# Local correlation on tiles of 8 rows by 16 columns instead of 4 whole rows

## The chip, the cores and the metric

The kernel runs on one core of a Trainium2 chip. The metric is the device time of one execution in microseconds; less is better. The times and the profile are of single executions; the table below has both.

## The reference

Eight images of 512 channels and 32x32 pixels go through two layers. With v = groupnorm(x), 32 groups of 16 channels:

```python
norm = sqrt(sum(v * v, axis=1, keepdims=True))
fn = v / maximum(norm, 1e-12)
fp = pad(fn, 2 pixels on each side)
vol = stack([sum(fp[:, :, r:h + r, cc:w + cc] * fn, axis=1)
             for cc in range(5) for r in range(5)], axis=1)     # 25 channels
x = x + relu(einsum('bihw,oi->bohw', concat([v, vol], axis=1), conv_w) + conv_b)
```

So each pixel is multiplied with its 25 neighbours over 512 channels, the 25 products are divided by the two norms, and a 1x1 convolution takes 512 + 25 channels to 512. All is float32.

## The kernel before

The work is 16 units, one image in one layer each (`ORDER`); four units lie in a ring of operand tiles. `KT` = 4 tiles of 128 channels, `PIX` = 1024 pixels. A float32 value is held as two float16 parts, high and low, so a convolution matmul is done three times (L442: `wh` with high, `wl` with high, `whh` with low). The order on every engine is written out by hand, and semaphores join them. In step k the engines do:

- TensorE: the correlation products of unit k (L453 to L472), then for the convolution of unit k-1 eight groups g of 12 matmuls with 512 columns (`channels`, L442) and one volume product (`volume`, L449), which adds the 25 correlation channels. The volume products of g = 0 and 1 come behind the 24 matmuls of these groups, since `vol` is late (`HOLD` = 1). At g = 2 stands the group average for unit k+1 (L420), at g = 4 the turning of unit k's neighbours (L494).
- ScalarE: eviction of the correlation products to `band` (L556), `vol` high part (L544), and between the ReLUs (L594) the high parts of unit k+1 (L536, from g = 2) and half of the turned rows (L587).
- VectorE: statistics of unit k+1 (`unit_stats`, L625), the low part of `vol` of unit k-1 (L689), the affine values (`unit_affine`, L646 to L670) at g = 0, norms and neighbours of unit k (L696 to L720) at g = 2, then per g one tile of unit k+1: `v` (L678) and the low part (L683). After each g's part comes the residual addition (L792). The copy of the other half of the turned rows (L728) comes at g = 4 behind the tile t = 2.
- SP: `band` to DRAM, and back skewed into `skew` (L284); outputs and new x tiles; the turned rows to DRAM (L289).
- GpSimd: three views of these rows from DRAM (L359 to L365) and three products with them (L378 to L383), whose result `corr` becomes `vol`.

The correlation works so: a block is 128 pixels, 4 whole rows. Its pixels are the weights (128 columns of `opnd`, high part); the moving operand is the 4 rows with 2 more above and below, 8 x 32 = 256 columns, with high and low part, for 4 channel tiles: 8 matmuls per block, 64 per unit. In the result [pixel, column] pixel i needs columns i to i + 132. `band` goes to DRAM row by row and is read back with a step one longer than a row, so that each partition gets its own window of `REACH` = 133 values for each of 8 blocks. `nbr` takes 25 of them and 25 mirrored ones; the borders of the image are rid of later through the padded rows.

GpSimd clears what is never written (L332 to L337); all engines wait for these constants.

Of the kernel before, what the change touches and what calls it, by code (L numbers as in the profile page):

```python
# [61 lines left out]
def build(nc, x, w0, b0, w1, b1, out):  # L62
# [8 lines left out]
    ROWS = P // WI  # L71
    BLOCKS = PIX // P
    BAND = (ROWS + 2 * R) * WI
    PAIRS = BLOCKS // 2
    REACH = 2 * R * WI + S
    CENTRE = R * WI + R
# [6 lines left out]
    GPAD = 64  # L83
    GSZ = GPAD + BLOCKS * P * BAND + GPAD
    GROUPS = 2 * KT
    BN = 6
    assert (B, UNITS) == (BATCHES, B * LAYERS) and BAND * 2 == HALF
# [7 lines left out]
    with ctx:  # L95
        def sb(name, shape, dt):
            return ctx.enter_context(nc.sbuf_tensor(name, shape, dt))
# [20 lines left out]
        band = sb("band", [P, PAIRS, HALF], F32)  # L118
# [39 lines left out]
        pads_out = sem("pads_out")  # L158
# [15 lines left out]
        low = sem("low")  # L174
        gram = sem("gram")
# [17 lines left out]
        CONSTS = 11  # L193
# [21 lines left out]
        def valid(u):  # L215
            return 0 <= u < UNITS

# [19 lines left out]
        def _(sp):  # L237
# [35 lines left out]
            def band_through_dram(k, q):  # L273

                for p in range(PAIRS):
                    sp.wait_ge(band_sb, PAIRS * k + p + 1)
                    dst = bass.AP(band_dram, q * GSZ + GPAD + 2 * p * P * BAND,
                                  [[BAND, P], [P * BAND, 2], [1, BAND]])
                    sp.dma_start(dst, band[:, p, :].rearrange("p (a n) -> p a n", a=2)).then_inc(band_out, 16)
# [3 lines left out]
                src = bass.AP(band_dram, q * GSZ + GPAD - R, [[BAND + 1, P], [P * BAND, BLOCKS], [1, REACH]])  # L283
# [34 lines left out]
        def _(pool):  # L318
# [14 lines left out]
            pool.memset(band[:, 0, 0:R * WI], 0.0).then_inc(const_step, 1)  # L333
            pool.memset(band[:, PAIRS - 1, HALF - R * WI:HALF], 0.0).then_inc(const_step, 1)
# [78 lines left out]
        def _(pe):  # L413
# [38 lines left out]
            def step(k, k0, i):  # L452
                if valid(k0):  # L453
                    slot = k0 % RING
                    pe.wait_ge(high, KT * (k + 1))
                    pe.wait_ge(low, KT * (k + 1))
                    if k0 == 2:
                        pe.wait_ge(w_low, W_LOWS * LAYERS)
                    for p in range(PAIRS):
                        wait(pe, band_sb, PAIRS * k + p - 1)  # L460
                        for j in range(2 * p, 2 * p + 2):
                            r0 = max(ROWS * j - R, 0)
# [354 lines left out]
```

## Time and profile before

| | |
|---|---|
| median of 3 runs | 570.47 us (570.29 to 570.53) |
| the profiled execution | 571.38 us, its span 569.5 us |
| TensorE granted clock, mean | 0.974 |
| busy: TensorE, VectorE, ScalarE, GpSimd | 502.5, 408.0, 258.7, 165.4 us |
| DMA | 69.43 MB, mean 122 GB/s |

The span is from the first to the last instruction. In the rows below, "PE" is TensorE's matmuls, "PEld" its weight loads, "DVE" VectorE, "ACT" ScalarE, "POOL" GpSimd, "SPq" the queue of SyncE that issues DMAs; L12 is line 12 of the kernel. A matmul's shown duration holds the pipeline's latency: the distance from start to start is what one costs. A busy share says nothing of what sets the end; that is in the chain and in the waits.

### The profile page before, as it was taken

To read this page: it belongs to the slowest core of one execution; us is meant where nothing else is said; L and a number is where in the kernel's file an instruction comes from. 1 tells how busy PE (TensorE), PEld (TensorE's weight loads), DVE (VectorE), ACT (ScalarE), POOL (GpSimd) and SP (SyncE) were. 2 spreads that over 40 slices of the span, in tenths; PEclk is the share of its full clock that TensorE was granted. 3 is DMA by queue.
4 is the path that set the end of the run, shared out by engine and by line. 5 is a ranking of instruction groups with operands and counts; after the bars stand their busy time and mean duration, and the time that the engine had idled before them with its cause. 6 is when DMAs were issued, how large, how long until landed. Compare 5 with 4: busy or idle time off the path is not lost.

```text
span 569.5 us, 7778 instructions
## 1 busy us (share of the span) xinstructions
PE 502.5 (88%) x2888; PEld 284.8 (50%) x2888; DVE 408.0 (72%) x828; ACT 258.7 (45%) x350; POOL 165.4 (29%) x135
## 2 busy tenths in 40 slices
PE   0357779999999989998999989998999989998996
PEld 0246337454564646454464636455464646454442
DVE  4879696786869588785969588785958778572442
ACT  1343454644546363643545364543646263543332
POOL 3354625023140504114140503214040503214240
PEclk9976989999999989999999989999999999999999
DMA  8764202223133812455043712356041512334403
GB/s 332 265 208 129 70 1 75 73 54 95 30 117 138 262 43 73 132 199 186 14 133 122 268 54 72 114 199 206 9 137 75 181 39 71 114 121 136 145 37 148
DMA packets 49885, 69.43 MB, mean 122 GB/s; under 512 B 6248, under 2 KB 39016, under 8 KB 49848
## 3 DMA queue, kind: packets, MB, share of 16 engines
q1 hardware_dynamic: 46008, 63.42, 33.1%
q0 software_dynamic: 3840, 5.52, 4.1%
q8 instruction: 23, 0.38, 0.3%
q14 instruction: 14, 0.11, 0.1%
HBM read 33.21 MB, written 35.71 MB: 121 GB/s over the span
## 4 chain that ended last, share of the span: by engine, by line
PE 34%; DVE 23%; issue 14%; POOL 14%; DMA 9%; ACT 5%; DVEq 0%; POOLq 0%
PE conv_ps L442 24%; DVE xs L792 5%; PE gram_ps L467 5%; DMA xs<-in_x_dram 4%; POOL corr L383 3%; POOL mirror L378 3%; DVE v L678 3%; POOL corr L381 3%; PE conv_ps L449 3%; DMA rows_dram<-rows 3%; DVE vol L689 2%; ACT act_out L594 2%; DMA out_dram<-xs 2%; DVE opnd L683 2%; DVE stats L625 2%
## 5 line engine op out<-in xcount | busy, mean ns | idle before, releaser
L442 PE MATMUL conv_ps<-opnd,wh 128*128 128x512 f16 x512 | 195.9, 383 | 0.2 <-ACT act_out L594 0.2
L442 PE MATMUL conv_ps<-opnd,whh 128*128 128x512 f16 x512 | 196.0, 383 | 0.0
L442 PE MATMUL conv_ps<-opnd,wl 128*128 128x512 f16 x512 | 195.9, 383 | 0.0
L594 ACT ACTIVATE act_out<-conv_ps,bias,wdown 128x512 f32<-128x512 f32 x128 | 97.4, 773 | 118.9 <-PE conv_ps L449 117.5
L792 DVE TENSOR_TENSOR xs<-xs,act_out 128x512 f32<-128x512 f32 x128 | 92.2, 736 | 44.8 <-ACT act_out L594 44.5
L467 PE MATMUL gram_ps<-opnd 128*128 128x256 f16 (+1 forms) x1024 | 111.1, 271 | 13.7 <-DVE opnd L683 11.7
L467 PEld LDWEIGHTS gram_ps<-opnd 128*128 128x128 f16 x1024 | 98.8, 100 | 27.6 <-issue 14.2
L625 DVE BATCH_NORM_STATS2 stats<-xs 128x6 f32<-128x512 f32 x128 | 78.3, 679 | 25.1 <-DMA xs<-in_x_dram 19.1
L359 POOL DMA_DIRECT2D mirror<-rows_dram x16 | 10.5, 659 | 273.3 <-DMA rows_dram<-rows 273.3
L683 DVE SCALAR_TENSOR_TENSOR opnd<-opnd,v 128x1024 f16<-128x1024 f16 x64 | 80.8, 1266 | 10.3 <-POOL v L390 4.1
L442 PEld LDWEIGHTS conv_ps<-opnd,whh 128*128 128x128 f16 x512 | 50.3, 98 | 61.8 <-issue 2.1
L536 ACT ACTIVATE opnd<-xs,affine 128x1024 f16<-128x1024 f32 x64 | 78.2, 1230 | 4.9 <-DVE affine L670 4.9
L442 PEld LDWEIGHTS conv_ps<-opnd,wh 128*128 128x128 f16 x512 | 51.5, 101 | 56.6 <-issue 2.1
L442 PEld LDWEIGHTS conv_ps<-opnd,wl 128*128 128x128 f16 x512 | 50.4, 98 | 56.3 <-issue 2.1
L556 ACT ACTIVATE band<-gram_ps 128x448 f32<-128x448 f32 (+1 forms) x64 | 36.5, 571 | 74.1 <-PE gram_ps L467 74.1
L449 PE MATMUL conv_ps<-vol,wvol 96*128 96x512 f16 x128 | 45.9, 381 | 17.3 <-DVE vol L689 14.4
L544 ACT ACTIVATE vol<-corr 25x1024 f16<-25x1024 f32 x32 | 33.8, 1055 | 51.4 <-POOL corr L383 51.0
L378 POOL TENSOR_TENSOR mirror<-mirror,rn_own 25x1024 f32<-25x1024 f32 x16 | 37.7, 2357 | 60.4 <-DMA rn_own<-rows_dram 60.4
L689 DVE SCALAR_TENSOR_TENSOR vol<-corr,vol 25x1024 f16<-25x1024 f32 x16 | 19.8, 1236 | 40.1 <-ACT vol L544 39.9
L678 DVE TENSOR_SCALAR v<-xs,affine 128x1024 f32<-128x1024 f32 x56 | 45.4, 811 | 0.0
L383 POOL TENSOR_TENSOR corr<-corr,mirror 25x1024 f32<-25x1024 f32 x16 | 37.9, 2366 | 1.3
L381 POOL TENSOR_TENSOR corr<-rows,rn_far 25x1024 f32<-25x1024 f32 x16 | 32.9, 2058 | 0.0
(67 smaller groups left out, 245.9 us busy)
## 6 DMA issues: line engine op xcount, KB each, us to landing
xs<-in_x_dram SPq DMA_DIRECT2D x32, 512.0 KB, 4.7
band_dram<-band SPq DMA_DIRECT2D x64, 256.0 KB, 2.3
out_dram<-xs SPq DMA_DIRECT2D x32, 512.0 KB, 2.9
skew<-band_dram SPq DMA_DIRECT2D x16, 532.0 KB, 4.0
opnd<-in_L_conv_conv_w_dram SPq DMA_DIRECT2D x2, 1074.0 KB, 12.5
rows_dram<-rows SPq DMA_DIRECT2D x16, 131.6 KB
mirror<-rows_dram POOLq DMA_DIRECT2D x16, 112.1 KB, 2.3
rn_far<-rows_dram POOLq DMA_DIRECT2D x16, 112.1 KB, 3.8
```

The lines of the kernel that those rows point to most:

```text
L378: pool.tensor_tensor(mir, mir, near, ALU.mult).then_inc(corr_step, 1)
L381: pool.tensor_tensor(dst, own, far, ALU.mult).then_inc(corr_step, 1)
L383: pool.tensor_tensor(dst, dst, mir, ALU.add).then_inc(corr_step, 1)
L442: pe.matmul(conv_ps[:, g % 4, :], w[:, l, t, m * P:(m + 1) * P], opnd[:, slot, part, t, n * HALF:(n + 1) * HALF], start=(t == 0 and w is w ...
L449: pe.matmul(conv_ps[:, g % 4, :], wvol[0:96, l, m * P:(m + 1) * P], vol[0:96, n * HALF:(n + 1) * HALF], start=False, stop=True).then_inc(c ...
L467: last = pe.matmul(gram_ps[:, p % 2, at:at + (r1 - r0) * WI], opnd[:, slot, 0, t, j * P:(j + 1) * P], opnd[:, slot, part, t, r0 * WI:r1 * WI],
L536: act.activation(opnd[:, u0 % RING, 0, t, :], xt, ACT.Identity, bias=affine[:, 0, 1, t:t + 1], scale=affine[:, 0, 0, t:t + 1]).then_inc(hi ...
L594: act.activation(act_out[:, g % 2, :], conv_ps[:, g % 4, :], ACT.Relu, bias=bias[:, l, m:m + 1], scale=wdown[:, l, m:m + 1]).then_inc(relu, 1)
L625: last = dve.bn_stats(stats[:, t, h, :], xs[:, slot, t, h * HALF:(h + 1) * HALF])
L678: dve.tensor_scalar(v2[:, t % 2, :], xs[:, ring_slot(unit_batch(k0 + 1) + 2 * i), t, :], affine[:, 1, 0, t:t + 1], affine[:, 1, 1, t:t + 1 ...
L683: dve.scalar_tensor_tensor(out=opnd[:, slot, 1, t, :], in0=opnd[:, slot, 0, t, :], scalar=-2.0, in1=v2[:, t % 2, :], op0=ALU.mult, op1=ALU ...
L792: dve.tensor_tensor(xt, xt, act_out[:, g % 2, :], ALU.add).then_inc(x_sum, 1)
```

## The change

A block becomes a tile of 8 rows by 16 columns: 4 tiles down, 2 across, still 8 blocks and 64 matmuls. The moving operand is 12 rows of 18 columns (`HELD`: 16 and 2 on the inner side; the other side is the image's border), 216 columns, or 180 at the upper and lower edge, picked from the image with a step of 32. [...] `band` holds 12 x 20 values per tile with zeros at the border, all of it cleared at the start. In DRAM the two tiles of a pair lie beside each other, 480 values per pixel, with pitches such that pixel i again reads with a constant step; each window is 85 values. The four writes of pads to DRAM go. ScalarE's eviction, the turning's target (L494) and the neighbour step (L717) follow the layout. The reserve for DMA descriptors is cut to 4096 bytes per partition, which makes room for `strips`.

```diff
+    TR, TC = 8, 16
+    DOWN, ACROSS = HI // TR, WI // TC
+    BLOCKS = DOWN * ACROSS
+    BR, BC = TR + 2 * R, TC + 2 * R
+    BAND = BR * BC
+    PAIRS = DOWN
+    REACH = 2 * R * BC + S
+    WL_PITCH = BLOCKS * BAND + 4
+    HL_PITCH = TC * (WL_PITCH + 1) - BC
+    GSZ = TR * HL_PITCH + TC
+    HELD = TC + R
...
+        strips = sb("strips", [P, KT, ACROSS, HI * TC], F16)
...
-            for q in range(2):
-                sp.dma_start(band_dram[q:q + 1, 0:GPAD], rows[0:1, 0:GPAD]).then_inc(pads_out, 16)
-                sp.dma_start(band_dram[q:q + 1, GSZ - GPAD:GSZ], rows[0:1, 0:GPAD]).then_inc(pads_out, 16)
-            sp.wait_ge(pads_out, 64)
...
-                    dst = bass.AP(band_dram, q * GSZ + GPAD + 2 * p * P * BAND,
-                                  [[BAND, P], [P * BAND, 2], [1, BAND]])
+                    dst = bass.AP(band_dram, q * GSZ + p * ACROSS * BAND,
+                                  [[HL_PITCH, TR], [WL_PITCH, TC], [1, ACROSS * BAND]])
...
-                src = bass.AP(band_dram, q * GSZ + GPAD - R, [[BAND + 1, P], [P * BAND, BLOCKS], [1, REACH]])
+                src = bass.AP(band_dram, q * GSZ, [[WL_PITCH + 1, P], [BAND, BLOCKS], [1, REACH]])
...
-            pool.memset(band[:, 0, 0:R * WI], 0.0).then_inc(const_step, 1)
-            pool.memset(band[:, PAIRS - 1, HALF - R * WI:HALF], 0.0).then_inc(const_step, 1)
+            pool.memset(band[:, :, :], 0.0).then_inc(const_step, 1)
...
+                    pe.wait_ge(stripped, KT * (k + 1))
...
-                                    last = pe.matmul(gram_ps[:, p % 2, at:at + (r1 - r0) * WI],
-                                                     opnd[:, slot, 0, t, j * P:(j + 1) * P],
-                                                     opnd[:, slot, part, t, r0 * WI:r1 * WI],
+                                    last = pe.matmul(gram_ps[:, p % 2, c * HALF // 2:c * HALF // 2 + HELD * (r1 - r0)],
+                                                     strips[:, t, c, p * P:(p + 1) * P],
+                                                     image(opnd[:, slot, part, t, :])[:, r0:r1, c0:c0 + HELD],
...
-                        act.activation(band[:, p, a:z], gram_ps[:, p % 2, a:z], ACT.Copy).then_inc(band_sb, 1)
+                        r0, r1 = held_rows(p)
+                        bp, gp = band[:, p, :], gram_ps[:, p % 2, :]
+                        dst = bass.AP(bp.tensor, bp.offset + (r0 - (p * TR - R)) * BC + R,
+                                      [list(bp.ap[0]), [BAND - R, ACROSS], [BC, r1 - r0], [1, HELD]])
+                        src = bass.AP(gp.tensor, gp.offset,
+                                      [list(gp.ap[0]), [HALF // 2, ACROSS], [HELD, r1 - r0], [1, HELD]])
+                        act.activation(dst, src, ACT.Copy).then_inc(band_sb, 1)
...
                 dve.wait_ge(high, KT * u + t + 1)
+                wait(dve, gram, PAIRS * u)
+                dve.tensor_copy(strips[:, t, :, :].rearrange("p c (h w) -> p c h w", w=TC),
+                                opnd[:, slot, 0, t, :].rearrange("p (h c w) -> p c h w", c=ACROSS, w=TC)
+                                ).then_inc(stripped, 1)
                 dve.wait_ge(twice, KT * u + t + 1)
...
-    nc = _bacc.Bacc("TRN2", target_bir_lowering=False, num_devices=1)
+    nc = _bacc.Bacc("TRN2", target_bir_lowering=False, num_devices=1, dynamic_dma_scratch_size=4096)
```

## Rows read from the trace of the kernel before

**Rows 1.** The page: engines' busy time (section 1) and the chain's shares (section 4).

```profile
PE 502.5 (88%) x2888; PEld 284.8 (50%) x2888; DVE 408.0 (72%) x828; ACT 258.7 (45%) x350; POOL 165.4 (29%) x135
PE 34%; DVE 23%; issue 14%; POOL 14%; DMA 9%; ACT 5%; DVEq 0%; POOLq 0%
```

**Rows 2.** Chain of work in time: start us, us, what, number.

```profile
92.94 6.56 PE gram_ps L467 x64
...
350.21 6.56 PE gram_ps L467 x64
```

**Rows 3.** Waits, 92 to 524 us: engine, line, releaser: total us, times, longest.

```profile
PE conv_ps L449 <- DVE vol L689: 14.4, 11, 2.7
```

**Rows 4.** Timeline of VectorE, one round: start, us, instruction [idle before, releaser].

```profile
457.28 1.21 DVE L689 SCALAR_TENSOR_TENSOR vol<-corr,vol 25x1024 f16<-25x1024 f32 x1 [3.33 <-ACT vol L544]
459.39 0.17 DVE L646 COPY gmv<-turn_ps 128x8 f32<-128x8 f32 x1 [0.90 <-PE turn_ps L420]
...
465.42 0.81 DVE L678 TENSOR_SCALAR v<-xs,affine 128x1024 f32<-128x1024 f32 x1
466.33 1.22 DVE L683 SCALAR_TENSOR_TENSOR opnd<-opnd,v 128x1024 f16<-128x1024 f16 x1
467.47 0.68 DVE L792 TENSOR_TENSOR xs<-xs,act_out 128x512 f32<-128x512 f32 x1
...
472.78 0.68 DVE L728 COPY rows<-turn_ps 90x512 f32<-90x512 f32 x1
...
488.62 1.21 DVE L689 SCALAR_TENSOR_TENSOR vol<-corr,vol 25x1024 f16<-25x1024 f32 x1 [3.33 <-ACT vol L544]
```

**Rows 5.** Windows: length, busy PE, PEld, DVE, ACT, POOL (instructions), clock, DMA.

```profile
461.90:473.50 11.60, 11.03 (x56) 5.30 (x54) 10.84 (x21) 8.11 (x10) 0.00 (x0) 1.00 0.00 0
```

**Rows 6.** Timeline of VectorE at the end of a round with an x load.

```profile
197.39 1.29 DVE L625 BATCH_NORM_STATS2 stats<-xs 128x6 f32<-128x512 f32 x2 [1.94 <-DMA xs<-in_x_dram]
...
199.64 1.22 DVE L689 SCALAR_TENSOR_TENSOR vol<-corr,vol 25x1024 f16<-25x1024 f32 x1
```

**Rows 7.** Timeline of TensorE: the first volume products of three rounds.

```profile
167.84 0.59 PE L449 MATMUL conv_ps<-vol,wvol 96*128 96x512 f16 x2 [0.70 <-DVE vol L689]
...
201.00 0.59 PE L449 MATMUL conv_ps<-vol,wvol 96*128 96x512 f16 x2 [2.18 <-DVE vol L689]
...
523.61 0.59 PE L449 MATMUL conv_ps<-vol,wvol 96*128 96x512 f16 x2 [2.67 <-DVE vol L689]
```

**Rows 8.** Prices: first eight correlation matmuls (timeline); L678 (groups by shape: busy, mean ns).

```profile
123.69 0.82 PE L467 MATMUL gram_ps<-opnd 128*128 128x192 f16 x8
...
L678 DVE TENSOR_SCALAR v<-xs,affine 128x1024 f32<-128x1024 f32 x56 | 45.4, 811 | 0.0
```

**Rows 9.** Timeline of GpSimd and VectorE at the start.

```profile
2.33 1.18 POOL L332 MEMSET rows<- 90x1296 f32 x1
3.45 0.15 POOL L333 MEMSET band<- 128x64 f32 x1
...
5.80 4.85 DVE L625 BATCH_NORM_STATS2 stats<-xs 128x6 f32<-128x512 f32 x8 [5.80 <-POOL nbr L337]
...
16.11 3.25 DVE L683 SCALAR_TENSOR_TENSOR opnd<-opnd,v 128x1024 f16<-128x1024 f16 x2 [1.44 <-POOL v L390]
```

**Rows 10.** The skewed read: page's DMA issues (KB, us to landing), timelines of SP and VectorE.

```profile
skew<-band_dram SPq DMA_DIRECT2D x16, 532.0 KB, 4.0
...
200.10 0.36 SPq L284 DMA_DIRECT2D skew<-band_dram  x1
...
205.47 0.16 DVE L696 TENSOR_SCALAR nsq<-skew 128x8 f32<-128x8 f32 x1
...
454.63 0.36 SPq L284 DMA_DIRECT2D skew<-band_dram  x1
```

**Rows 11.** Windows behind two of these waits, columns as in rows 5 (clock: third from the end).

```profile
201.90:205.30 3.40, 3.40 (x10) 1.21 (x8) 2.62 (x13) 1.05 (x3) 0.00 (x0) 0.50 0.45 136
...
523.60:527.00 3.40, 3.39 (x16) 1.57 (x17) 1.82 (x6) 1.66 (x3) 0.00 (x0) 1.00 0.00 0
```

More of the change, by code:

```diff
@@ L82, in build @@
     MIR = (HI - 1) * PW + WI
-    GPAD = 64
-    GSZ = GPAD + BLOCKS * P * BAND + GPAD
+    WL_PITCH = BLOCKS * BAND + 4
+    HL_PITCH = TC * (WL_PITCH + 1) - BC
+    GSZ = TR * HL_PITCH + TC
+    HELD = TC + R
     GROUPS = 2 * KT
     BN = 6
-    assert (B, UNITS) == (BATCHES, B * LAYERS) and BAND * 2 == HALF
+    assert (B, UNITS) == (BATCHES, B * LAYERS) and BAND * 2 <= HALF and ACROSS == 2 and TR * TC == P
     weights = (w0, w1)
@@ L115, in build @@
         wvol = sb("wvol", [P, LAYERS, C], F16)
+        strips = sb("strips", [P, KT, ACROSS, HI * TC], F16)
         vol = sb("vol", [P, PIX], F16)
         v2 = sb("v2", [P, 2, PIX], F32)
-        band = sb("band", [P, PAIRS, HALF], F32)
+        band = sb("band", [P, PAIRS, ACROSS * BAND], F32)
         skew = sb("skew", [P, BLOCKS, REACH], F32)
@@ L174, in build @@
         low = sem("low")
+        stripped = sem("stripped")
         gram = sem("gram")
@@ L191, in build @@
         x_sum = sem("x_sum")
-        CONSTS = 11
+        CONSTS = 10
         BN_STEPS = KT + KT + 2
@@ L216, in valid, with image, held_rows @@
             return 0 <= u < UNITS
+        def image(a):
+            return a.rearrange("p (h w) -> p h w", w=WI)
+        def held_rows(p):
+            return max(p * TR - R, 0), min((p + 1) * TR + R, HI)
         def w_turned_at(l, n):
@@ L460, in step @@
                         wait(pe, band_sb, PAIRS * k + p - 1)
-                        for j in range(2 * p, 2 * p + 2):
-                            r0 = max(ROWS * j - R, 0)
-                            r1 = min(ROWS * (j + 1) + R, HI)
-                            at = (j % 2) * BAND + (r0 - (ROWS * j - R)) * WI
+                        r0, r1 = held_rows(p)
+                        for c in range(ACROSS):
+                            c0 = 0 if c == 0 else WI - HELD
                             for t in range(KT):
                                 for part in range(2):
-                                    last = pe.matmul(gram_ps[:, p % 2, at:at + (r1 - r0) * WI],
-                                                     opnd[:, slot, 0, t, j * P:(j + 1) * P],
-                                                     opnd[:, slot, part, t, r0 * WI:r1 * WI],
+                                    last = pe.matmul(gram_ps[:, p % 2, c * HALF // 2:c * HALF // 2 + HELD * (r1 - r0)],
+                                                     strips[:, t, c, p * P:(p + 1) * P],
+                                                     image(opnd[:, slot, part, t, :])[:, r0:r1, c0:c0 + HELD],
                                                      start=(t == 0 and part == 0),
@@ L493, in step @@
                         for j in range(BLOCKS):
-                            last = pe.transpose(turn_ps[0:NROWS, j * P // HALF, j * P % HALF:j * P % HALF + P],
+                            h, c = j // ACROSS, j % ACROSS
+                            last = pe.transpose(image(turn_ps[0:NROWS, h // 2, :])[:, h % 2 * TR:(h % 2 + 1) * TR,
+                                                                                  c * TC:(c + 1) * TC],
                                                 nbr[:, j, :], ident[:, :])
```

15 lines of the change are left out of this document (4 added, 11 removed).

## The prediction

> **What bounds the kernel now.** I read the page first. TensorE is busy 88% of the span and VectorE 72%, but of the chain that ended last TensorE has only 34%, VectorE 23%, GpSimd 14% and DMA 9% [rows 1]: a loop over several engines ends the rounds, not TensorE's work alone. Next the chain in order of time. A correlation block of 64 matmuls (L467) should stand on it 16 times if its length mattered in every unit; it stands there four times (23.96, 92.94, 221.15 and 350.21 us), the second and the last shown in [rows 2]. Then the waits between 92 and 524 us: TensorE waits in 11 rounds for vol of L689 before it can do the volume product L449 [rows 3].
>
> So I followed one round on VectorE [rows 4]. L689 at 457.28 writes vol, TensorE does L449 and the group average, and from the copy L646 at 459.39 VectorE has a queue that hardly breaks: affine steps, two residual additions, norms, neighbours, then tiles of the next unit (L678, L683, one addition L792 each), and only behind the third tile, at 472.78, the copy of turned rows L728. Between 461.9 and 473.5 it is busy 10.84 us of 11.60, the rest being the gaps between dependent small steps [rows 5]. The copy ends at 473.46. Then comes a leg without a TensorE matmul in it: rows to DRAM, three views back, three GpSimd products, ScalarE's vol, until L689 starts at 488.62, 15.16 us later. The round is 31.34 us: 2.11 + 14.07 + 15.16. L467 is in none of the three parts. TensorE runs beside it, and waits for it.
>
> There is a second kind of round: four in which a new x tile is loaded. There the last loads hold the statistics (L625), and L689 stands behind these in VectorE's queue [rows 6]. Such a round, from L449 at 167.84 to L449 at 201.00 [rows 7], has 33.16 us, with TensorE waiting 2.18 us at its end. The path is TensorE's products, output, load, statistics. The correlation block is not on it either: it runs beside the output and the load.
>
> **The change part by part.**
>
> *Correlation matmuls.* Columns per unit: before 48 of 256 and 16 of 192, 15360. After 12 rows of 18 are 216, at the upper and lower edge 10 rows of 18 are 180: 32 x 216 + 32 x 180 = 12672. 64 matmuls in 6.56 us [rows 2] are 102.5 ns each, and the first eight of 192 columns take 0.82 us with their tail [rows 8]; both fit one column per 1/2.4 ns plus 2.5 ns. So the block becomes 32 x 92.5 + 32 x 77.5 ns = 5.44 us, a saving of 1.12 us per unit, 17.9 us over 16 units. By the above it is worth nothing where TensorE waits for vol; it is worth 1.1 us at unit 2 (92.94), a few tenths for the first unit, and lengthens the wait elsewhere. Bounds: 192-column matmuls are the shortest of their kind here; if 180 costs as much as 192 (82.5 ns) the saving is 0.96. That strided runs of 18 are slower shows nowhere and is a rival.
>
> *The strips.* Four new VectorE copies per unit, 128x1024, f16 to f16, each between L678 and L683 of its tile. The nearest row by size and by its single tensor source is L678: 811 ns, f32 [rows 8]. The floor is the 128x8 copy L646, 170 ns [rows 4]. Half the bytes of L678: 170 + (811 - 170) / 2 = 490 ns, an estimate, which I take. What it adds is less. L683 waits for L678 today: it starts 0.91 us after it though L678 has 0.81 [rows 4], and independent neighbours overlap by 0.08 us (L683 has 1.22 and the next addition starts 1.14 later). Tile now: 0.91 to L683. Tile then: 0.73 + 0.41 = 1.14. So +0.23 us per copy; +0 at the floor, +0.55 at 811 ns, and +0.97 at 1.22 us, the duration of L683 at one element per cycle. Three of the four stand ahead of L728, in a queue with no slack: +0.7 us per round. The fourth is hidden: VectorE later waits for ScalarE and for vol.
> The Trainium skill, "VectorE: DVE Perf Modes", perf-mode tier table, gives a 16-bit copy within SBUF four elements per cycle. By it I estimate 0.42 us per copy, 0.16 added, 0.5 per round, and a total 2 us lower than below. No row here has a 16-bit VectorE copy.
>
> The rounds it counts in are those whose L689 waits for the leg behind L728. From unit 2 to unit 14 there are thirteen; four are load rounds, and a load round has room against a plain one (33.16 beside 31.34: 1.8 us) that takes up 0.7. Nine rounds x 0.7 = 6.3 us. The tail behind unit 14 has no next unit, no copy and no correlation block: 0.
>
> *Start.* The two small clears of band (0.15 us each, L333, L334) become one of 1920 f32 per partition. L332 clears 1296 in 1.18 us, so 1.75 us, 1.45 more. The first statistics wait for these constants with all x tiles there (idle 5.80, then eight without a break) [rows 9]: +1.45, all of it on the path. SP loses the four pads and their landing, ahead of load(2), whose tiles are not waited for: 0. In units 0 and 1 GpSimd computes v beside VectorE, and there L683 takes 3.25 us for two instead of 2.4 [rows 4, 9]: the engines get in each other's way. The copies partly fill idle time and partly wait behind GpSimd: between 0 and 3 us over both units, I take 1.0. The four tiles of unit 2 stand on the chain behind 66.7 us: +0.9, against the 1.1 of unit 2's shorter block: 0 together.
>
> *Eviction and DMA.* L556 writes 432 and 360 columns instead of 512 and 448, in the shadow of the block: 0. Band goes out as 1920 B per partition instead of twice 1024; skew comes back in 1024 chunks of 340 B instead of 532. Skew lands after 4.0 us, the median [rows 10]. In a plain round it is issued at 454.63 and has landed when the affine steps begin at 459.39, and the norms come behind these [rows 4, 10]. Behind a load round it is issued at 200.10 and read at 205.47: 1.4 us of room. I take no change: 0; double would cost there (rival). The smaller reserve for descriptors touches three small GpSimd DMAs per unit: 0, bounds -0.3 to +0.3 us per unit.
>
> *The clock.* TensorE's wait at L449 grows in plain rounds by 1.1 + 0.7 us, in load rounds by 1.1. Granted clock after a wait of 2.18 us: 0.50 for 3.4 us; after one of 2.67 us at 523.61: 1.00 [rows 7, 11]. So a wait of over 2 us may or may not halve the clock (1.2 instead of 2.4 GHz), which costs 1.7 us of TensorE's time. Where the next wait swallows that it is free. It isn't at unit 14: the wait becomes 4.5 us, and TensorE is the bound from there to the end: +1.7. In each of four load rounds it could cost 1.7 as well, if the plain round before it ends in a halved clock: 0 to 6.8, in the range only.
>
> Sum on the profiled execution (569.5 span, 1.9 around it, 571.4): 1.45 + 1.0 + 0 + 6.3 + 1.7 = +10.4, so 581.8. The median is 0.9 under the profiled run: **581.0**.
>
> **The rivals.**
> 1. *The copy is slow*, one element per cycle (1.22 us). For: 16-element pieces from two interleaved halves. Price: 9 x 2.9 in plain rounds, 4 x 1.1 in load rounds, 3.9 less 1.1 at unit 2, 5 for the start and the clock: 38 us, 609 with the 0.9 off. 0.10.
> 2. *Strided matmuls are slow.* If a column costs double, the block takes 10.9 us, 4.3 more than now; TensorE's 0.4 to 0.7 of wait goes and every round grows by 3.7: 13 x 3.7 + 3 = 51 on 570.5, 621. Against: the rows of 36 bytes are read in order. 0.05.
> 3. *Skew's small chunks.* If the landing doubles to 8 us, the four rounds behind loads lose 4.0 - 1.4 = 2.6: +10, 591. The Trainium skill, "DMA: Bandwidth & Descriptors", Specifications, wants 512 B per transfer for full rate, with read-modify-write below it; 532 is above and 340 below, so by that rule this rival holds. Against: a third less data. 0.08.
> 4. *Faster.* The copy vanishes in the gap in which L683 waits for L678, and the shorter block counts where TensorE or shared DMA time sets the end: first unit -0.3, unit 2 -1.1, four load rounds -0.8 each with less band traffic beside the load, against 1.45: -3.2, 567. It decides if a copy adds under 0.05 us. If, besides, TensorE were the real bound in all rounds, 553. Against: the waits of [rows 3]. 0.05.
>
> **How the numbers follow.** Forecast 0.67, rivals 0.28, the rest (GpSimd at the start, descriptors) 0.05. Copy at its floor, with nothing for the clock or the crowding at the start: 1.45 less 1.1 on 570.5, 571; with both, 574. Copy at 811 ns: 9 x 1.65 + 1.1 (unit 2) + 1.45 + 3 + 1.7 = 22.1, 593. Range 574 to 594, which holds the forecast with its clock terms and rival 3; rivals 1, 2 and 4, 0.20 together, are outside. Differences under about 0.2% (1.1 us) can't be told from none. Faster 0.07 (rival 4 and a part of the rest), same 0.05 (the copy at its floor or below), slower 0.88.
>
> **What would show it.** Right: 5.4 us for the 64 matmuls of a unit; copies of 0.4 to 0.5 us; the copy of turned rows 0.5 to 0.7 us later behind L646; a longer wait for vol at the volume product; first statistics 1.45 later; load rounds of the same length. Wrong: matmuls that take more than their columns, a copy of turned rows that is not later, norms that wait for skew, or a correlation block on the chain in most units.

## The result, and the profile after

The changed kernel takes 584.06 us (median of 4 runs, 581.12 to 584.57) against 570.5 us: 1.0219 times the kernel before, interval 1.0179 to 1.0260. On another chip it was 1.0205 (1.0175 to 1.0235), against a median of 571.69 us there. The forecast was 581.0, range 574 to 594, slower. The profiled execution took 584.57 us with a span of 582.5, so the two spans differ by 13.0 us.

The page of the changed kernel: section 1, the granted clock by slice, the chain's shares, and three groups of section 5.

```profile
PE 495.4 (85%) x2888; PEld 280.7 (48%) x2888; DVE 421.6 (72%) x892; ACT 255.0 (44%) x350; POOL 170.0 (29%) x134
...
PEclk9986899999999989997999989998999989997999
...
DVE 31%; POOL 19%; PE 18%; issue 15%; DMA 9%; ACT 6%; SPq 1%; DVEq 0%; POOLq 0%
...
L456 PE MATMUL conv_ps<-vol,wvol 96*128 96x512 f16 x128 | 47.0, 391 | 32.6 <-DVE vol L706 31.3
...
L696 DVE COPY strips<-opnd 128x1024 f16<-128x1024 f16 x64 | 26.9, 420 | 3.2 <-ACT opnd L545 3.2
...
skew<-band_dram SPq DMA_DIRECT2D x16, 340.0 KB, 3.3
```

TensorE's share of the chain went from 34% to 18% [rows 1], and VectorE's and GpSimd's rose, from 23% to 31% and from 14% to 19%. Its wait for vol at the volume product (L456 now, L449 before) went from 14.4 us in 11 waits [rows 3] to 31.3 in 13. The correlation block stands on the chain in time only twice now (four times before, [rows 2]):

```profile
97.05 5.52 PE gram_ps L474 x64
...
190.63 5.54 PE gram_ps L474 x64
```

So it shrank from 6.56 us to 5.53, which over 16 units is 16.5 us, and the wait for vol grew by 16.9. The change does what it says on TensorE, and all of it is waited away again. TensorE's busy time fell by 7.1 us only (502.5 to 495.4), since more of its work ran at the half clock: the mean granted clock went from 0.974 to 0.957.

VectorE in a plain round of the changed kernel, the timeline; L706 is L689 before, L659 is L646, L745 is L728, L691 is L678, L700 is L683, and L696 is the new copy of a channel tile's high part into `strips`, from which TensorE now takes its weights.

```profile
432.95 1.21 DVE L706 SCALAR_TENSOR_TENSOR vol<-corr,vol 25x1024 f16<-25x1024 f32 x1 [3.33 <-ACT vol L553]
435.06 0.17 DVE L659 COPY gmv<-turn_ps 128x8 f32<-128x8 f32 x1 [0.90 <-PE turn_ps L427]
...
438.78 0.16 DVE L713 TENSOR_SCALAR nsq<-skew 128x8 f32<-128x8 f32 x1
...
441.12 0.80 DVE L691 TENSOR_SCALAR v<-xs,affine 128x1024 f32<-128x1024 f32 x1
441.84 0.42 DVE L696 COPY strips<-opnd 128x1024 f16<-128x1024 f16 x1
442.17 1.22 DVE L700 SCALAR_TENSOR_TENSOR opnd<-opnd,v 128x1024 f16<-128x1024 f16 x1
443.31 0.68 DVE L809 TENSOR_TENSOR xs<-xs,act_out 128x512 f32<-128x512 f32 x1
...
448.90 0.68 DVE L745 COPY rows<-turn_ps 90x512 f32<-90x512 f32 x1
...
466.35 1.22 DVE L706 SCALAR_TENSOR_TENSOR vol<-corr,vol 25x1024 f16<-25x1024 f32 x1 [3.51 <-ACT vol L553]
```

From the start of L659 to that of L745 it is 13.84 us; from L646 to L728 it was 13.39 [rows 4]: +0.45 for three copies. A tile takes 1.05 us from L691 to L700 (442.17 less 441.12) and not 0.91, so a copy adds 0.14 to 0.15 us though it has 0.42: it fills part of the gap in which L700 waited for L691.

Where the 13.0 us came from, by the start of the first volume product of each unit in the timelines of TensorE. The last column is from the trace of the same kernel on the other chip, with a span of 584.0 us:

| Stretch | before | after | difference | second trace |
|---|---|---|---|---|
| start to unit 0 | 66.73 | 70.20 | +3.47 | +4.28 |
| unit 0 to 1 | 37.79 | 37.63 | -0.16 | +0.01 |
| nine plain rounds, 1 to 14 | 287.84 | 292.46 | +4.62 | +6.33 |
| four load rounds, 3-4, 5-6, 7-8, 9-10 | 131.25 | 133.58 | +2.33 | +1.32 |
| unit 14 to the end | 45.84 | 48.62 | +2.78 | +2.6 |

So one trace fixes the size of a stretch to no better than 1 to 2 us.

### The profile page after: what moved, and what is told of

Read it like the earlier page. It is cut to its first block, busy times and chain, and to the rows that moved or that the text cites. A ratio compares the mean times of both kernels' runs of the same rounds, so it can differ in the third digit from the quotient of the medians.

```text
span 582.5 us, 7851 instructions
## 1 busy us (share of the span) xinstructions
PE 495.4 (85%) x2888; PEld 280.7 (48%) x2888; DVE 421.6 (72%) x892; ACT 255.0 (44%) x350; POOL 170.0 (29%) x134
## 3 DMA queue, kind: packets, MB, share of 16 engines
q1 hardware_dynamic: 37296, 59.22, 31.1%
## 4 chain that ended last, share of the span: by engine, by line
DVE 31%; POOL 19%; PE 18%; issue 15%; DMA 9%; ACT 6%; SPq 1%; DVEq 0%; POOLq 0%
PE conv_ps L449 13%; DVE opnd L700 6%; DVE xs L809 5%; POOL mirror L385 5%; POOL corr L390 5%; DVE v L691 4%; POOL corr L388 4%; DMA rows_dram<-rows 4%; DMA band_dram<-band 3%; ACT vol L553 2%; DVE vol L706 2%; ACT act_out L607 2%; PE gram_ps L474 2%; PE conv_ps L456 2%; DVE stats L638 2%
## 5 line engine op out<-in xcount | busy, mean ns | idle before, releaser
L449 PE MATMUL conv_ps<-opnd,wh 128*128 128x512 f16 x512 | 199.8, 390 | 0.2 <-ACT act_out L607 0.2
L449 PE MATMUL conv_ps<-opnd,whh 128*128 128x512 f16 x512 | 199.2, 389 | 0.0
L449 PE MATMUL conv_ps<-opnd,wl 128*128 128x512 f16 x512 | 199.0, 389 | 0.0
L809 DVE TENSOR_TENSOR xs<-xs,act_out 128x512 f32<-128x512 f32 x128 | 88.4, 708 | 43.9 <-ACT act_out L607 43.9
L474 PE MATMUL gram_ps<-opnd,strips 128*128 128x180 f16 (+1 forms) x1024 | 94.3, 253 | 15.3 <-DVE opnd L700 15.3
L474 PEld LDWEIGHTS gram_ps<-opnd,strips 128*128 128x128 f16 x1024 | 91.7, 98 | 19.6 <-issue 15.8
L449 PEld LDWEIGHTS conv_ps<-opnd,whh 128*128 128x128 f16 x512 | 51.0, 100 | 64.3 <-issue 6.5
L700 DVE SCALAR_TENSOR_TENSOR opnd<-opnd,v 128x1024 f16<-128x1024 f16 x64 | 79.6, 1244 | 1.9 <-POOL v L397 1.9
L449 PEld LDWEIGHTS conv_ps<-opnd,wh 128*128 128x128 f16 x512 | 52.6, 103 | 58.6 <-issue 5.4
L449 PEld LDWEIGHTS conv_ps<-opnd,wl 128*128 128x128 f16 x512 | 51.2, 100 | 58.6 <-issue 6.0
L456 PE MATMUL conv_ps<-vol,wvol 96*128 96x512 f16 x128 | 47.0, 391 | 32.6 <-DVE vol L706 31.3
L569 ACT ACTIVATE band<-gram_ps 128x360 f32<-128x360 f32 (+1 forms) x64 | 32.4, 507 | 62.1 <-PE gram_ps L474 62.1
L706 DVE SCALAR_TENSOR_TENSOR vol<-corr,vol 25x1024 f16<-25x1024 f32 x16 | 19.8, 1236 | 43.4 <-ACT vol L553 43.3
L691 DVE TENSOR_SCALAR v<-xs,affine 128x1024 f32<-128x1024 f32 x56 | 45.5, 812 | 0.0
L456 PEld LDWEIGHTS conv_ps<-vol,wvol 96*128 96x128 f16 x128 | 11.6, 98 | 51.3 <-ACT vol L553 29.9
## 6 DMA issues: line engine op xcount, KB each, us to landing
opnd<-in_L_conv_conv_w_dram SPq DMA_DIRECT2D x2, 1074.0 KB, 12.8
```

The costliest lines, as they stand in the source:

```text
L449: pe.matmul(conv_ps[:, g % 4, :], w[:, l, t, m * P:(m + 1) * P], opnd[:, slot, part, t, n * HALF:(n + 1) * HALF], start=(t == 0 and w is w ...
L456: pe.matmul(conv_ps[:, g % 4, :], wvol[0:96, l, m * P:(m + 1) * P], vol[0:96, n * HALF:(n + 1) * HALF], start=False, stop=True).then_inc(c ...
L474: last = pe.matmul(gram_ps[:, p % 2, c * HALF // 2:c * HALF // 2 + HELD * (r1 - r0)], strips[:, t, c, p * P:(p + 1) * P], image(opnd[:, sl ...
L691: dve.tensor_scalar(v2[:, t % 2, :], xs[:, ring_slot(unit_batch(k0 + 1) + 2 * i), t, :], affine[:, 1, 0, t:t + 1], affine[:, 1, 1, t:t + 1 ...
L700: dve.scalar_tensor_tensor(out=opnd[:, slot, 1, t, :], in0=opnd[:, slot, 0, t, :], scalar=-2.0, in1=v2[:, t % 2, :], op0=ALU.mult, op1=ALU ...
L809: dve.tensor_tensor(xt, xt, act_out[:, g % 2, :], ALU.add).then_inc(x_sum, 1)
```

## The experiments

Ratios are to the kernel before on the same chip, over five rounds each, with their interval. Names of lines are those of the kernel from which the edit starts.

### The parts of the change alone

**The clear of band.** The kernel before, with the first of its two small clears made 1920 f32 long:

```diff
-            pool.memset(band[:, 0, 0:R * WI], 0.0).then_inc(const_step, 1)
+            pool.memset(band[:, :, :].rearrange('p a n -> p (a n)')[:, 0:1920], 0.0).then_inc(const_step, 1)
```

> The kernel before, with one edit: the first clear of band writes 1920 float32 values per partition, as the change does, instead of 64. Nothing else changes. Theory: the constants are done about 1.45 us later, the first statistics of VectorE start at 7.25 us instead of 5.80, and all of it reaches the end: 572.0 us. Rival: the x tiles or the weights set the start, and the time stays at 570.5.

Measured 1.0039 (1.0012 to 1.0067), about 2 us, with the first volume product 1.59 us later. In the changed kernel the same is seen on GpSimd and VectorE (timelines), 1.47 us later than in [rows 9]:

```profile
3.45 1.70 POOL L341 MEMSET band<- 128x1920 f32 x1
...
7.27 4.85 DVE L638 BATCH_NORM_STATS2 stats<-xs 128x6 f32<-128x512 f32 x8 [7.27 <-POOL nbr L344]
```

**The copies.** The kernel before, with the four copies in front of L683 and the smaller descriptor reserve; nothing reads the strips, and the correlation matmuls are the old ones:

```diff
                 dve.wait_ge(high, KT * u + t + 1)
+                wait(dve, gram, PAIRS * u)
+                dve.tensor_copy(strips[:, t, :, :].rearrange("p c (h w) -> p c h w", w=16),
+                                opnd[:, slot, 0, t, :].rearrange("p (h c w) -> p c h w", c=2, w=16)
+                                ).then_inc(stripped, 1)
...
+                    pe.wait_ge(stripped, KT * (k + 1))
```

> The kernel before with the four copies per unit into strips added on VectorE, at the place where the change has them, and the smaller reserve for DMA descriptors; the copies are waited for and not used, the correlation block keeps its 4-row blocks. Theory (VectorE's queue ahead of the copy of turned rows sets the round): 0.42 us per copy, 0.14 us added each, the copy of turned rows 0.4 us later behind the group average in every round, nine plain rounds x 0.4 = 3.8 us, and 2 to 3 us at the start, where the copies meet GpSimd's work: 576 to 577 us, TensorE's wait for vol longer by 0.4 in plain rounds. Rival (TensorE's own work is the bound, or the copies fall into gaps): within 1 us of 570.5.

Measured 1.0173 (1.0137 to 1.0210), 9.9 us, where 6 were expected. The copies take 422 ns here (groups by shape):

```profile
L686 DVE COPY strips<-opnd 128x1024 f16<-128x1024 f16 x64 | 27.0, 422 | 3.2 <-ACT opnd L539 3.2
```

The first volume product comes 1.85 us later, units 1 to 14 take 423.3 us instead of 419.1 (2.5 us of it in the nine plain rounds, 1.7 in the load rounds), and the tail 47.54 instead of 45.84: a fall of the clock behind unit 14's wait, which the expectation didn't have. So the copies alone make most of the slowdown; with the clear it is 2.1%. The shorter block, the new stores and the new read together come to about nothing, within some 3 us by these intervals.

**The copies moved behind the queue.** The changed kernel, with the copies of tiles 0 to 2 behind the copy of turned rows (L745) from unit 2 on:

```diff
...
+                    last_copied = TURN_AT(k0) if k0 > 1 else -1
+                    if 0 <= t < KT and valid(k0 + 1) and g > last_copied:
+                        strip_tile(k, k0, t)
+                    if g == last_copied and valid(k0 + 1):
+                        for s in range(t + 1):
+                            strip_tile(k, k0, s)
```

> The changed kernel with the same four VectorE copies per unit, but from the third step on those of tiles 0 to 2 stand behind the copy of turned rows instead of ahead of it. No work is taken away. Theory (only the queue ahead of that copy counts): the copy of turned rows ends 14.8 to 14.9 us behind the volume product instead of 15.3, nine plain rounds become 0.4 us shorter, 3 to 4 us in all: 580 to 581 us. Rival (it is the amount of VectorE work, wherever it stands): no change, 584.

Measured 1.0092 (1.0058 to 1.0125), a median of 576.5 us, 4 us lower than expected. From the first volume product to the turned rows' end it is 14.85 us again in most rounds (15.27 in the changed kernel, 14.82 before), units 1 to 14 take 421.0 us, and the tail is 45.87 us: the clock did not fall there, which the expectation had left out. So it is their place in the queue that costs, more than their 27 us of work. Over the clear's 2 us some 3 are left; in the trace the plain rounds are as short as before (287.3 us for 287.84) and the load rounds 2.5 us longer.

**ScalarE copies the strips.** The changed kernel with the four copies on ScalarE, two groups of the convolution later than the tile's high part:

```diff
+                act.wait_ge(high, KT * u + t + 1)
+                act.activation(strips[:, t, :, :].rearrange("p c (h w) -> p c h w", w=TC),
+                               opnd[:, u0 % RING, 0, t, :].rearrange("p (h c w) -> p c h w", c=ACROSS, w=TC),
+                               ACT.Copy).then_inc(stripped, 1)
...
-                dve.tensor_copy(strips[:, t, :, :].rearrange("p c (h w) -> p c h w", w=TC),
```

> The changed kernel with the four copies into strips on ScalarE instead of VectorE, 1.2 us each, from the third step on two groups later than the tile, in gaps where ScalarE waits for TensorE. Theory: the copy of turned rows ends 14.8 us behind the volume product again, nine plain rounds lose 0.4 us each and the start 1 to 2 us: 4 to 6 us less than the changed kernel, ratio to the kernel before 1.012 to 1.015. Rival (the copy itself costs little, the rest of the change is what is slow): ratio 1.02 as for the changed kernel.

Measured 1.0044 (1.0018 to 1.0069), where 1.012 to 1.015 was expected. A copy takes 1048 ns on ScalarE, and yet the kernel is 1.7% faster than with 420 ns on VectorE. The clear, and in the trace a tail of 47.55 us, are most of what is left over the kernel before.

### Is TensorE hidden, and what is its saving worth?

**The queue's last tile moved.** In both kernels the copy of turned rows (L728, L745) is put ahead of the third tile of the next unit, not behind it:

```diff
-                    if k0 == 0 and g == TURN_AT(k0):
+                    if (k0 == 0 or k0 > 1) and g == TURN_AT(k0) and valid(k0):
                         first_rows(k)
...
-                    if k0 != 0 and g == TURN_AT(k0) and valid(k0):
+                    if k0 == 1 and g == TURN_AT(k0) and valid(k0):
```

> The kernel before with one move: from the third step on VectorE's copy of turned rows stands ahead of tile t = 2 instead of behind it, so ahead of one v step and one low step (0.91 + 1.14 us). Theory (the round is: VectorE's queue up to this copy, then the leg through DRAM, GpSimd and ScalarE): the copy ends 12.8 us behind the volume product instead of 14.8, TensorE's wait for vol vanishes in plain rounds and these shrink from 31.6 to TensorE's own 30.8 us; load rounds stay at 32.4 to 33.2. Nine x 0.8 = 7 us less: ratio 0.988. Rival (TensorE's work or the DMA sets all rounds already): ratio 1.00.

> The changed kernel with the same move of the copy of turned rows ahead of tile t = 2 (and its strips copy). Theory (the shorter correlation block is worth something only where TensorE is the bound): the copy ends 12.9 us behind the volume product, TensorE becomes the bound of plain rounds with 29.8 us, one less than in the kernel before with this move; nine rounds x 2.0 us less than the changed kernel, and fewer falls of the clock: 562 to 566 us where the kernel before has 570.5, ratio 0.985 to 0.992, 2 to 4 us under the kernel before with this move (nine us won by the block, less 3.4 at the start and longer waits in load rounds). Rival (the change is slow for another reason, the matmuls or DMA): it stays 10 us above the kernel before with this move.

Measured: the kernel before with it 0.9816 (0.9782 to 0.9850), better than the 0.988 expected, the changed kernel with it 0.9926 (0.9898 to 0.9954). I had expected the changed kernel to come out lower of the two, by 2 to 4 us; it is 6 us above. The waits of TensorE at the volume product, the former kernel first, then the latter:

```profile
PE conv_ps L449 <- DVE vol L689: 7.3, 5, 2.0
```

```profile
PE conv_ps L456 <- DVE vol L706: 20.3, 14, 3.8
```

In the kernel before, TensorE waited for vol in seven of the nine plain rounds, 0.4 to 0.7 us in five of them. With turned rows 2.04 us sooner (14.82 to 12.78 behind the volume product) most plain rounds are 30.81 us long with no wait for vol, so that is TensorE's own work. Four of the five waits left are those of rounds that end with an x load; the fifth is 0.2 us at unit 14. In the changed kernel TensorE would need 29.8 (an estimate, 30.81 less the 1.03 of the block), but the median of its plain rounds is 31.1: first volume product to turned rows is 13.08 us and not 12.78, and behind that GpSimd's part begins later. Its DMA issue of mirror takes 1108 ns there in the mean and 659 in the kernel before (groups of lines, the changed kernel with the edit first):

```profile
L366 POOL DMA_DIRECT2D mirror<-rows_dram x16 | 17.7, 1108 | 262.4 <-DMA rows_dram<-rows 262.4
```

```profile
L359 POOL DMA_DIRECT2D mirror<-rows_dram x16 | 10.5, 659 | 273.3 <-DMA rows_dram<-rows 273.3
```

It isn't that VectorE is busy: it is busy all through the issue in the two kernels without the edit as well, and there the mean is 659 and 658 ns, with the copies and without them. What differs is the instruction that runs beside it. In those two it is the low part and an addition. With the edit it is `v`, and in the changed kernel the copy behind it. GpSimd's and VectorE's timelines of the changed kernel with the edit:

```profile
154.72 1.62 POOL L366 DMA_DIRECT2D mirror<-rows_dram  x1 [17.90 <-DMA rows_dram<-rows]
...
155.10 0.80 DVE L691 TENSOR_SCALAR v<-xs,affine 128x1024 f32<-128x1024 f32 x1
155.82 0.41 DVE L696 COPY strips<-opnd 128x1024 f16<-128x1024 f16 x1
```

The issue ends at 156.34, 0.11 us behind the copy (156.23). In the kernel before with the edit, where `v` stands alone, such an issue takes 1.14 us and ends 0.11 us behind `v`; the others take 0.65. This holds in six rounds of each of the two kernels with the edit; in the combination below one issue beside the start of `v` took 0.65 us all the same. So a longer issue goes with `v` and the copy beginning beside it. That they hold it up is read from these times, and no run tests it by itself.

**Both moves.** The changed kernel with the strips on ScalarE, the turned rows ahead of the third tile, and the clear of band behind the other constants, with only the first eviction waiting for it:

```diff
-            pool.memset(band[:, :, :], 0.0).then_inc(const_step, 1)
...
             pool.memset(nbr[:, :, NS:BACK], 0.0).then_inc(const_step, 1)
+            pool.memset(band[:, :, :], 0.0).then_inc(const_step, 1)
...
-            dve.wait_ge(const_step, CONSTS)
+            dve.wait_ge(const_step, CONSTS - 1)
...
+                            if k0 == 0:
+                                act.wait_ge(const_step, CONSTS)
```

> The changed kernel with three edits: the copies into strips on ScalarE, the copy of turned rows ahead of tile t = 2, and the clear of band as the last of GpSimd's constants, for which only ScalarE waits, ahead of its first band. Theory: the start comes back by 1.45 and 1 to 2 us, TensorE is the bound of plain rounds with 29.8 us: 558 to 562 us where the kernel before has 570.5, ratio 0.98 to 0.985. Rival (with TensorE at the bound the band's slower way through DRAM, 4.8 to 5.4 us from the last store's issue to the skewed read's instead of 2.1, takes its place): ratio above 0.99, norms that wait for skew in plain rounds.

Measured 0.9720 (0.9686 to 0.9753), better than the 0.98 to 0.985 expected, and 0.9744 (0.9714 to 0.9775) when it ran again on another chip, some 557 us. It beats both kernels, and the kernel before with its turned rows moved (562.7) by 5 us. Its chain (the page) has TensorE at half:

```profile
PE 52%; DMA 16%; DVE 14%; issue 6%; POOL 6%; ACT 4%; SPq 1%; DVEq 0%; POOLq 0%; ACTq 0%
```

Plain rounds at its start take 29.96 and 30.11 us, below the 30.81 that TensorE needs with the old block. Of the kernels run, only this one has time from the smaller block.

### The clock

**Dummy matmuls ahead of the wait.** The changed kernel with eight matmuls of 512 columns, whose result nobody reads, in front of TensorE's wait for vol:

```diff
                     if g == hold:
+                        if k0 > 2:
+                            pe.wait_ge(rows_a, k)
+                            for _ in range(WARM):
+                                pe.matmul(turn_ps[:, 1, :], wh[:, 0, 0, 0:P], opnd[:, slot, 0, 0, 0:HALF],
+                                          start=True, stop=True)
                         pe.wait_ge(vol_high, 2 * (u + 1))
```

> The changed kernel, with eight more matmuls of 512 columns on TensorE ahead of the wait for vol in each round from the third on; they write a bank that nothing reads then (a result of no use) and wait for ScalarE's copy of it, done long before. They take 1.7 us of the 2.0 to 4.8 us in which TensorE waits there. Theory (the waits make the granted clock fall to 0.50 behind six of the rounds): no fall behind these rounds, the last round of 31.28 us comes back to about 28.5, the plain rounds behind load rounds lose 0.4 to 0.9: 4 to 6 us less than the changed kernel, 578 to 580 us. Rival (the clock costs nothing, the loads vary): the same time as the changed kernel, or more where the eight matmuls are longer than the wait.

Measured 1.0241 (1.0197 to 1.0284): missed. The half clock behind the waits was gone but for one, but in unit 15, where TensorE is the bound, the dummies themselves stood in the way (1.73 us). So once more with none in that unit (`if 2 < k0 < UNITS`), beside the changed kernel itself:

> The changed kernel once more, unchanged, so that the next two runs have it on the same chip. Both theories: 1.022 times the kernel before (about 584 us), nine plain rounds of 31.8 to 32.1 us and a last full round (units 14 to 15) of 31.3 us with the matmuls of turn T and of the correlation block partly at half clock.

> The changed kernel with eight dummy matmuls (512 columns each, to a PSUM tile that nobody reads) ahead of the wait for vol, from unit 3 to unit 14 and none in the last step, where TensorE is the bound. Theory A, the fall of the clock behind unit 14's wait costs 2.8 us in the last full round: no half clock there, V14 to V15 28.5 instead of 31.3, and a few tenths behind each load round, 3 to 4 us under the changed kernel, near 580. Theory B, the clock is free, because the norms' wait for skew and the queues set the rounds: within 1 us of the changed kernel, and what the last round gains is lost before.

Measured 1.0205 (1.0175 to 1.0235) without and 1.0214 (1.0175 to 1.0253) with dummies: medians of 583.67 and 583.99 us. Windows behind the wait of unit 14, in the changed kernel as profiled first, and with the dummies:

```profile
532.70:539.50 6.80, 5.63 (x14) 2.09 (x15) 4.27 (x11) 2.51 (x4) 0.00 (x0) 0.50 0.27 99
```

```profile
532.70:539.50 6.80, 5.17 (x24) 2.36 (x25) 4.71 (x12) 3.73 (x6) 0.00 (x0) 1.00 0.40 127
```

In the traces it does what it should: clock 1.00 for 0.50, unit 14 to the end 45.86 us instead of 48.46 in the trace beside it, while unit 14 starts within 1.2 us. In the medians nothing of it is left. The runs of either spread over 4 to 6 us, and a gain of 2.6 may lie in it. That the other executions had no half clock to lose is unlikely: the mean granted clock is 0.948 to 0.960 in all six without dummies and 0.964 to 0.980 in all six with them. Where the time goes instead stays open. The theory that the clock is worth 3 to 4 us of median is not borne out.

### The stores of band

The stores are fewer bytes than before and are slower. SP's timeline in one plain round of the kernel before and of the changed one (the DMAs out of band, then the skewed read, which waits for them):

```profile
126.00 5.38 SPq L279 DMA_DIRECT2D band_dram<-band  x4
133.15 0.36 SPq L284 DMA_DIRECT2D skew<-band_dram  x1
```

```profile
128.89 4.84 SPq L287 DMA_DIRECT2D band_dram<-band  x4
137.98 0.38 SPq L292 DMA_DIRECT2D skew<-band_dram  x1
```

From the end of the last issue to the read's issue it is 1.77 us before (133.15 - 126.00 - 5.38) and 4.25 after; from the last issue's start, 2.1 and 4.8. Over the span SP waits for these stores 39.6 us before, 76.9 after. Behind a round with an x load the skewed read comes so late that the norms wait for it, which they never did (SP's and VectorE's timelines):

```profile
206.11 0.38 SPq L292 DMA_DIRECT2D skew<-band_dram  x1
...
209.35 0.17 DVE L713 TENSOR_SCALAR nsq<-skew 128x8 f32<-128x8 f32 x1 [0.30 <-DMA skew<-band_dram]
```

The read lands 3.24 us after its issue there; [rows 10] had 5.37 from issue to norms.

How many engines carry the stores can be read from the DMA share, the mean busy share of the core's 16 DMA engines. Behind the changed kernel's stores it stays at half for 4 us (windows; the share is the number before the last):

```profile
133.00:137.00 4.00, 4.00 (x21) 1.78 (x19) 1.72 (x7) 0.13 (x1) 3.92 (x2) 1.00 0.48 150
```

```profile
131.80:132.60 0.80, 0.80 (x5) 0.35 (x4) 0.00 (x0) 0.00 (x0) 0.80 (x1) 1.00 0.87 296
```

The second is the kernel before at the end of its stores, where the share reaches 0.87 and 296 GB/s, against 0.48 and 150.

**Pixels in column order.** In the changed layout the outer dimension in DRAM is 8 rows (before it was the 128 pixels of a tile). The run is the combination above, with the pixels of a tile ordered by column, so that it is 16 columns; the same bytes in the same runs of 1920 B. The read back and the turning follow the order, and the pitches change a little (1920 values from pixel to pixel in the store's inner dimension for 1924):

```diff
                     dst = bass.AP(band_dram, q * GSZ + p * ACROSS * BAND,
-                                  [[HL_PITCH, TR], [WL_PITCH, TC], [1, ACROSS * BAND]])
+                                  [[WL_PITCH, TC], [HL_PITCH, TR], [1, ACROSS * BAND]])
...
-                act.activation(strips[:, t, :, :].rearrange("p c (h w) -> p c h w", w=TC),
+                for c in range(ACROSS):
+                    last = act.activation(
+                        strips[:, t, c, :].rearrange("p (k w h) -> p k h w", w=TC, h=TR),
```

> The combination (strips copied by ScalarE, turned rows copied ahead of the third tile, band cleared last) again, unchanged, as the neighbour of the next run. Both theories: 0.972 times the kernel before, the last band store's issue to the skewed read's issue 4.8 us or more, first volume product to turned rows 12.8 us in plain rounds and 13.1 to 14.0 behind load rounds.

> The combination with the pixels of a tile in column order, so that the band store's outer dimension in DRAM is 16 columns and not 8 rows; same bytes, same runs of 1920 B. Two ScalarE copies a tile instead of one. Theory A, the store is slow because only 8 of the 16 DMA engines carry it: last store's issue to skewed read's issue falls from 4.8 to 2.1 to 2.6 us, the norms behind load rounds don't wait for skew, first volume product to turned rows 12.8 us there too, and the total is 1 to 3 us lower than its neighbour's. Theory B, it is slow for where the rows lie in DRAM or for their length: it stays near 4.8 us and the total stays within 1 us, or rises by up to 2 us for the second ScalarE copy.

SP's waits for the stores, in the combination and in column order (total, times, longest), and the issues of column order:

```profile
SPq L292 <- DMA band_dram<-band: 75.8, 16, 6.6
```

```profile
SPq L294 <- DMA band_dram<-band: 37.7, 16, 2.9
...
band_dram<-band SPq DMA_DIRECT2D x64, 240.0 KB, 2.7
```

The wait is halved and its longest is 2.9 us, also behind load rounds; from the last issue's start to the read's it is 2.8 us in a plain round, where 2.1 to 2.6 was expected and 4.8 was before. Behind load rounds the norms no longer wait for skew, and first volume product to turned rows is 12.8 us there too; in the combination the norms wait in seven rounds, 3.2 us in all. So the length of the rows is not the cause; the outer dimension of 8 is what is left. The new order moves the rows in DRAM as well, and no run changes that alone; but the DMA share speaks for the engines. It was half in the changed kernel, and in column order it goes up to 0.84 with 229 GB/s (windows):

```profile
137.00:138.00 1.00, 1.00 (x6) 0.48 (x5) 1.00 (x1) 0.00 (x0) 1.00 (x1) 1.00 0.84 229
```

This fits what the Trainium skill, "DMA: Bandwidth & Descriptors", says in the section "Why a DMA increments its semaphore by 16 and not by 1": the number of DMA engines is the largest up to 16 that divides the slowest dimension of both sides. By that rule 8 of 16 engines carry a store with an outer dimension of 8, and the trace agrees: a share of 0.48, and a doubled wait. No row names the single engines.

What it would give the whole kernel couldn't be read: the run took 1.337 times the kernel before (1.3338 to 1.3402), for ScalarE's copies (group by shape):

```profile
L556 ACT ACTIVATE strips<-opnd 128x512 f16<-128x512 f16 x128 | 304.2, 2624 | 0.5
```

Two of 2624 ns a tile instead of one of 1048: they read runs of 16 elements as before, but write each element 16 bytes from the last. TensorE waits for them, and the total says nothing on the stores.

## Why the prediction was right, and where it wasn't

**Right.** The bound: VectorE's queue up to the turned rows, then the leg through DRAM, GpSimd and ScalarE, with TensorE waiting beside them. The experiments bear it out from both sides: 27 us of copies in the queue cost 9.9, the same copies elsewhere a fraction, and 16.5 us saved on TensorE gave nothing. Rivals 1, 2 and 4 fell: copies of 420 ns, 64 matmuls in 5.53 us (5.44 expected), a slower kernel. That the total lies only 3 us from the forecast is in part luck: the copies in plain rounds were put too high, and start, tail and stores too low.

**The terms.**

| Term | predicted | measured | second trace |
|---|---|---|---|
| clear | +1.45 | +1.47 | +1.47 |
| copies at the start | +1.0 | +2.0 (3.47 - 1.47); alone 1.85 | +2.8 |
| unit 2 | 0 | -0.16 (unit 0 to 1) | +0.01 |
| nine plain rounds | +6.3 | +4.6 | +6.3 |
| four load rounds | 0 (0 to 6.8) | +2.3 | +1.3 |
| tail, clock | +1.7 | +2.8 | +2.6 |
| sum | +10.4 | +13.0 | +14.6 |

*The copy.* Mis-sized: I took 490 ns and +0.23, and it is 420 and +0.14 to 0.15. The estimate from the page "VectorE: DVE Perf Modes" of the Trainium skill, perf-mode tier table, 0.42 us and 0.16 added, was the better one; the halved f32 row was the wrong neighbour for a 16-bit copy. Nine rounds times 0.45 are 4.1 us. In sum over the nine rounds the turned rows come 5.0 us later in the first trace and 5.7 in the second: most of what is over the 4.1 comes behind load rounds, where the stores delay the norms. So the 6.3 of the second trace meets the forecast by chance, with cheaper copies and a term that I had at zero.

*The start.* One to two us too low. The eight copies of units 0 and 1, beside GpSimd's work, add 2.0 to 2.8 us, where eight times the 0.15 of the loop are 1.2: within the bounds of 0 to 3 that I had.

*"I take no change"* for the stores was the step that failed. I weighed their bytes and their runs, which fell and stayed, and not what stands outermost in the target. Rival 3 had the right place, the norms behind load rounds, and the wrong mechanism: the read of 340 B chunks lands in 3.3 us, sooner than 4.0 for 532 B, so its doubled landing and its price of 10 us are not there. The 512 B rule of the Trainium skill, "DMA: Bandwidth & Descriptors", Specifications, can't be judged from these two, since the bytes fell by more (36%) than the time (18%). From the first store's issue to the read's it is 9.1 us in a plain round for 7.2 before, and 1.4 to 2.8 us more behind load rounds. There the room was 1.4, and the turned rows come up to 0.5 us later than in the rounds beside them, up to 0.6 in the second trace. By the sums above, in this kernel that is worth about 1 to 2 us, an estimate; in the faster combination the norms wait up to 1.6 us at once.

*Load rounds.* 2.1 of the 2.3 us lie in one, units 5 to 6, whose x load landed late (in the second trace 0.25 there, and 1.5 in units 9 to 10). Without the late load it is near the zero that I had taken.

*The clock.* At unit 14 TensorE waits 4.02 us by its timeline and then runs at 0.50 for 6.8 us, two times the 3.4 of [rows 11], so 2.8 us for 1.7:

```profile
533.87 1.01 PE L456 MATMUL conv_ps<-vol,wvol 96*128 96x512 f16 x2 [4.02 <-DVE vol L706]
```

In the traces this is the change turning against the kernel: it lengthens the wait, the clock is lower behind the wait, and where TensorE is the bound that is paid. Both parts of the change take part. With the copies and the old block the wait at unit 14 is 2.72 us, with the shorter block and the copies on ScalarE 3.19 us, and behind either the tail is 1.7 us longer than before. With the late copies the same wait is 1.78 us and the clock stays at 1.00. What of it the medians hold, the dummies left open.

The profiled run came out 2.6 us above the sum and the median 3 us above the forecast: in that trace start and tail each 1 us more, the load rounds 2 more, the plain rounds 1.7 less.

## What to carry to other kernels

Ask first where a saved engine's time would go: here 16.5 us of matmuls became 16.9 us of waiting, and the copies that paid for them stood in the one queue that sets the round. The same copy costs the kernel less on an engine 2.5 times slower at it if that engine isn't in the loop, and the saving counts only after the queue itself has been shortened. When a DMA's pattern is laid out anew, look at the size of its outermost dimension on both sides, and not only at bytes and run lengths.

## What the hardware showed that I had not expected

- A DRAM target with an outer dimension of 8 instead of 16 made SP wait 76 us rather than 38 for the same 64 stores of 240 KB, with a DMA share of 0.48 for 4 us behind them.
- ScalarE copies 1024 16-bit elements in 1.05 us when both sides are runs of 16, and needs 2.62 us for 512 when it writes them 16 bytes apart: 5.1 ns an element for 1.0.
- VectorE needs 0.42 us for the same 1024 in runs of 16, and adds 0.14 to a queue with a dependent gap in it.
- GpSimd's issue of a DMA takes 0.65 us beside VectorE's low part or addition, and 1.14 or 1.62 us when `v`, or `v` and the copy, begin beside it: it ends 0.11 us behind them, in six rounds of each of two kernels.
- A moving operand of TensorE in runs of 36 bytes cost next to nothing: 64 matmuls of 216 and 180 columns in 5.53 us, for 5.44 estimated from the old shapes.
- TensorE's granted clock was 0.50 for 6.8 us behind waits of 4.0 to 4.7 us in the changed kernel and for 3.4 us behind most of about 3. Between 2.1 and 2.7 us both occur: 0.50 behind 2.18 and 1.00 behind 2.67 in the kernel before [rows 7, 11]; with the late copies it was 1.00 behind 1.78.
